# The place of the v projection in slot 3 of a transformer layer on TensorE

## What is computed

```python
q = (route @ wq + bq).reshape(b_, r_, k_, H, D)
k = (route @ wk + bk).reshape(b_, r_, k_, H, D)
v = (route @ wv + bv).reshape(b_, r_, k_, H, D)
scores = jnp.einsum('brkhd,brnhd->brknh', q, k) / D ** 0.5
attn = jax.nn.softmax(scores, axis=3)
out = jnp.einsum('brknh,brnhd->brkhd', attn, v).reshape(b_, r_, k_, m_)
out = out @ wo + bo
x = _layernorm(route + out, ln1_g, ln1_b)
ff = jax.nn.relu(x @ w1 + b1) @ w2 + b2
return _layernorm(x + ff, ln2_g, ln2_b)
```

## Time and profile before

| | |
|---|---|
| runs of the kernel | 4436.37, 4440.16, 4438.13 us; median 4438.13 us |
| the profiled execution | 4437.33 us, its span 4435.3 us |
| mean granted TensorE clock | 0.990 of full speed |
| TensorE busy, matmuls | 97% of the span |
| TensorE busy, weight loads | 85% |
| VectorE busy | 85% |
| GpSimd busy | 81% |
| ScalarE busy | 77% |

### The profile page before, as it was taken

How to read it: one execution, slowest core, us unless ns; L and a number is a source line. 1 busy time by engine, 2 the same in 40 slices (tenths; PEclk the granted TensorE clock), 3 DMA queues, 4 the chain that set the end, 5 groups by cost and what they waited for, 6 DMA issues and landing times.

```text
span 4435.3 us, 151196 instructions
## 1 busy us (share of the span) xinstructions
PE 4316.3 (97%) x51984; PEld 3791.2 (85%) x51984; DVE 3748.7 (85%) x9739; ACT 3417.8 (77%) x5889; POOL 3613.0 (81%) x4620
## 2 busy tenths in 40 slices
PE   4999999999999999999999999999999999999998
PEld 4888888888888888888888888888888888888886
DVE  4888888888888888888888888888888888888886
ACT  2777777777777777777778777877777777777776
POOL 4788888878888888788888878888887888888887
PEclk7999999999999999999999999999999999999999
DMA  4444444444444444444444444444444444444442
GB/s 110 122 129 129 125 131 126 130 120 131 125 129 128 129 130 124 124 129 129 126 131 125 131 121 131 126 130 129 127 130 119 128 130 128 126 131 127 130 126 60
DMA packets 756258, 555.92 MB, mean 125 GB/s; under 512 B 95872, under 2 KB 755328, under 8 KB 755456
## 3 DMA queue, kind: packets, MB, share of 16 engines
q1 hardware_dynamic: 755456, 545.81, 45.6%
HBM read 69.47 MB, written 67.11 MB: 31 GB/s over the span
## 4 chain that ended last, share of the span: by engine, by line
PE 75%; issue 13%; DVE 6%; ACT 3%; SPq 2%; DMA 1%; DVEq 0%; POOL 0%; ACTq 0%; POOLq 0%
PE oT_ps L697 11%; PE bankB L656 10%; PE bankC L656 10%; PE bankC L635 10%; PE s_ps L670 9%; PE sT_ps L684 8%; PE bankA L710 5%; PE bankA L765 5%; DVE rest_sb L468 5%; PE bankB L635 4%; ACT nT_parts L425 3%; PE bankA L629 2%; SPq L238 1%; DMA stack<-parts 1%; SPq L210 0%
## 5 line engine op out<-in xcount | busy, mean ns | idle before, releaser
L390 ACT ACTIVATE prob_sb<-sT_ps 128x1024 f32<-128x1024 f32 x1024 | 1049.5, 1025 | 770.8 <-PE sT_ps L684 753.6
L498 DVE TENSOR_REDUCE max_sb<-s_ps 128x8 f32<-128x1024 f32 x1024 | 1230.5, 1202 | 24.8 <-PE s_ps L670 14.8
L263 POOL TENSOR_TENSOR parts<-rest_sb,parts 128x512 bf16<-128x512 f32 x512 | 584.1, 1162 | 266.0 <-ACT parts L364 266.0
L670 PE MATMUL s_ps<-stack 96*128 96x128 bf16 x8192 | 638.5, 221 | 31.3 <-issue 15.0
L670 PEld LDWEIGHTS s_ps<-stack 96*128 96x128 bf16 x8192 | 485.3, 98 | 209.8 <-issue 178.7
L684 PE MATMUL sT_ps<-stack 99*128 99x128 bf16 x8192 | 629.1, 219 | 1.3 <-ACT prob_sb L390 1.3
L697 PE MATMUL oT_ps<-prob_sb,v_ones 128*32 128x128 f32 x16384 | 554.0, 276 | 2.2 <-ACT prob_sb L390 2.2
L656 PE MATMUL bankB<-w_sb,h_sb 128*128 128x128 f32 x4096 | 513.1, 278 | 2.4 <-ACT h_sb L371 2.4
L684 PEld LDWEIGHTS sT_ps<-stack 99*128 99x128 bf16 x8192 | 504.3, 98 | 3.0 <-ACT prob_sb L390 1.8
L656 PE MATMUL bankC<-w_sb,h_sb 128*128 128x128 f32 x4096 | 499.2, 275 | 0.0
L635 PE MATMUL bankC<-nT_parts,w_parts 128*128 128x512 f32 x1536 | 467.0, 412 | 27.2 <-DVE rest_sb L468 4.9
(11 more groups left out here) (80 smaller groups left out, 9321.4 us busy)
## 6 DMA issues: line engine op xcount, KB each, us to landing
stack<-parts SPq DMA_DIRECT2D x3072, 128.0 KB, 2.4
x_sb<-in_x SPq DMA_DIRECT2D x256, 256.0 KB, 3.0
out<-out_sb SPq DMA_DIRECT2D x256, 256.0 KB, 2.3
stack<-max_parts SPq DMA_DIRECT2D x768, 8.0 KB, 1.9
w_sb<-in_L_conv_w SPq DMA_DIRECT2D x2, 256.0 KB, 3.1
be_row<-in_L_conv_ln_b SPq DMA_DIRECT2D x2, 256.0 KB, 19.9
g_row<-in_L_conv_ln_g SPq DMA_DIRECT2D x2, 256.0 KB, 22.7
bo_row<-in_L_conv_bo SPq DMA_DIRECT2D x1, 256.0 KB, 8.7
```

What stands on the lines that cost most here:

```text
L263: pool.tensor_tensor(parts[:, r % 2, 3 * c + LO], rest_sb[:, c], parts[:, r % 2, 3 * c + MID], ALU.subtract).then_inc(lo_split, 1)
L390: act.activation(prob_sb[:, s % 2], sT_ps[:], ACT.Exp, scale=float(D) ** -0.5).then_inc(exp_done, 1)
L498: dve.reduce_max(max_sb[:, (r - lag) % 2, :, s], s_ps[:].rearrange("p (h k) -> p h k", h=H), AX.X).then_inc(max_done, 1)
L670: ins = pe.matmul(s_ps[:, h * P:(h + 1) * P], stack[0:PROD, (r - lag) % 4, 0, h, tok], stack[0:PROD, (r - lag) % 4, 1, h, tok], start=True ...
```

## The change

In slot 3 the projection of v is written between the two chunks of the feed-forward, where it stood behind both. Nothing else differs; in the changed kernel v's products have the line 764 in place of 765.

```diff
--- before.py
+++ after.py
@@ -757,7 +757,6 @@
                                  ident[:]).then_inc(maxT_done, 1)
                 if live(t, r, 5):
                     hidden(t, r, 5, 0)
-                    hidden(t, r, 5, 1)
                 if live(t, r, 0):
                     pe.wait_ge(xT_joined, upto(t, r, 0, plus=1))
                     pe.wait_ge(rest_made, upto(t, r, 0, per=2, plus=1))
@@ -765,6 +764,8 @@
                         ins = pe.matmul(A[:, s * P:(s + 1) * P], xT_sb[:, s * P:(s + 1) * P],
                                         wv_sb[:], start=True, stop=True)
                     ins.then_inc(v_done, 1)
+                if live(t, r, 5):
+                    hidden(t, r, 5, 1)
                 if live(t, r, 3):
                     if live(t, r, 2):
                         pe.wait_ge(max_parts_made, upto(t, r, 2, plus=1))
```

## The result

| | before | changed |
|---|---|---|
| median of the runs | 4439.15 us (4436.37 to 4445.43, 4 runs) | 4361.82 us (4358.52 to 4365.66, 4 runs) |
| the profiled execution | 4437.33 us | 4365.66 us |
| its span | 4435.3 us | 4363.6 us |

The ratio is 0.9824 with a 95% interval of 0.9807 to 0.9841: 77 us faster. Forecast were 4350 us and a gain of 88.

A forecast was written before the change was run, and what follows sets the result against it. TensorE bounds the kernel, waiting at h1 for VectorE's remainder of k. 247 x 0.39 = 96 us less 8 for late landings is 88, so 4437.33 becomes 4349, plus 0.8: 4350 us; forecast range 4330 to 4372, 80% range 4322 to 4388.

The forecast's parts named there:

- h1's wait: TensorE, second feed-forward chunk: the remainder of k ends 0.45 us ahead of it, so its wait goes whole.
- v's own waits: TensorE, v between the chunks: remainder of q done some 0.3 us ahead, joined x over 4 us; no wait.
- The price of the wait: TensorE, first chunk's loads to attend's: 2.86 us with the wait, 2.49 without, so 0.37 us a step.
- Boundaries: TensorE, new changeovers v to h1 and h1 to attend: h0 to attend 2.47 us, gain 0.39 a step, bounds 0.10 and 0.49.
- The 0.02 taken off because of L710's row: h0 to attend taken as 2.47, not 2.49 us: v-shaped group to chunk shows no idle time before its loads.
- The upper bound of 2.76: h0 to attend, if h1 to attend costs the largest idle time after such a product, 0.27 us.
- What is late next: Spare left: slot 0's scores 0.20 us, x's transposes 0.21, h1's relu 0.1; late stack landings give back 8 us.
- the bubble was hidden anyway: Rival: h1's wait costs only the matmul rows' 4.9 us in all, giving 4433 us; chance 0.04.
- A wait takes its place: Rival: z, the maximum or landings hold TensorE in most steps; 0.2 us a step left, 4389 us; chance 0.13.
- The full gain: Rival: loads at both new boundaries hide behind running products; 0.49 us a step, about 4317 to 4325; chance 0.08.
- slower by a new boundary: Rival: TensorE's changeovers v to h1 and h1 to attend cost more than the bubble; 4463 us; chance 0.03.
- Both signs of failure: Wrong if z or L498 ends TensorE's idle time in most steps, or 0.3 us idle precedes h1 or attend.

The follow-up runs named there:

- e5: Kernel before, v still behind both chunks, with q and k exchanged on every engine so k comes first: 4354.55 us, ratio 0.9812.
- e6: Changed kernel with v ahead of both feed-forward chunks instead of between them: 4451.64 us, ratio 1.0032.
- e7: e1 with one filler memset a step on VectorE ahead of the row maximum of slot 3: 4356.03 us.
- e1: Changed kernel with the six stacking DMAs of the high parts issued early, ahead of the row maxima's DMAs: 4341.82 us, ratio 0.9779.
- e2: Kernel before with the six stacking DMAs of the high parts issued early, ahead of the row maxima's DMAs: 4429.39 us, ratio 0.9979.
- e4: Changed kernel without the middle and low parts of the row maxima's split, three VectorE instructions a step fewer: 4341.57 us, ratio 0.9777.

## Why the prediction was right, and where its sizes were off

The forecast of 4350 us missed the median of 4361.82 by 12, inside its range, with the sign and the mechanism it named. The ends of that range are looser than the prediction says: by its own terms, gains of 0.30 and 0.45 a step with 0 to 24 us of DMA lateness give 4388 and 4327, not 4372 and 4330. The measured time lies inside either.

1. *h1's wait* and *v's own waits*: right. The remainder of k was forecast 0.45 us ahead of h1 and was 0.57; v has no idle time before it. e5 shows that the gain comes with the wait gone and v in its old place, and e6 that v must not come before the remainder of q.

2. *The price of the wait.* Read from two neighbouring steps at 0.37 us, with the matmul row's 4.9 us and the load row's 134.3 us set aside. The loads now give 2.86 - 2.48 = 0.38, the chain 16.83 - 16.48 = 0.35 for the whole step. Behind attend the ordinary loads stand where they stood but for one hundredth (attend to L710's loads: 1.86 before, 1.87 now); over 500 to 4000 us the medians of h0 to attend are 2.85 and 2.49, so the 0.38 of two single steps is a little large. What the prediction cites there tells how near TensorE is to its limit. It prices no wait, and neither row was the price of this one.

3. *Boundaries*: mis-sized by a little. I took 2.47 and then a gain of 0.39 for the whole step; the order is worth 0.01 at most (e5), the step gains 0.35. That is 247 x 0.04 = 10 us of the 11 that were missing. The 0.02 taken off because of L710's row had no ground. The upper bound of 2.76 was far off, and the row, the same work in the same 2.49 us, was right. The Trainium skill's rule that loads are pulled ahead of running matmuls (TensorE: Matmul & The Clock Gate, Step-by-step), which would have given 0.49 a step, does not show here: attend's narrow loads start 0.37 us after the last load of h1, at 3012.03, when h1's products are all but through (the chain has them until 3012.10). The page ties the rule to row groups that do not conflict, or to the background weight buffer; no row here shows whether either held.

4. *What is late next*: all right in kind. The maximum was forecast 0.20 us ahead of slot 0's scores; the profile has 0.22, and e7's filler measures 0.21. z has 0.29, forecast 0.21. The stack's lateness was put at 8 us back, 20 steps of 0.4; e1 and e2 together show 10.5, and the table 18 waits of 10.4 us behind the first 200 us.

Sum with the measured terms: 247 x 0.35 = 86, less 10.5: 76, against 77 measured. The two terms that were off, 0.39 for 0.35 and 8 for 10.5, lean the same way. The agreement to 1 us is closer than the terms allow: 0.01 us a step is 2.5 us, and the medians of the kernel before differ by 1.9 us between sets.

Of the rivals, *the bubble was hidden anyway* falls with the result. *A wait takes its place* is true only for the landings and at 10.5 us; for VectorE it is not yet true, with 0.2 us in hand. *The full gain* and *slower by a new boundary* fall with 2.48 us from h0 to attend.

Both signs of failure that the prediction named came up, and both were badly chosen. The first was that L498 ends TensorE's idle time in most steps; the table now has that row 249 times, 60.0 us, where it had 39. But the idle time itself is the same 0.20 us before the scores of slot 0 as in the earlier trace rows, where it is called "issue". The maximum now ends 0.22 us ahead of these loads instead of 0.59, near enough for the profile to name it, and e7 shows that it is not yet what the loads wait for.

The second was an idle time of 0.3 us or more before attend; there are 0.37 us, put down to the maxima, and e4 shows that the maxima are not what it waits for. By the rows it is the time in which h1's wide products run out before attend's narrow loads start; no run changed the width of either, so this reading is not shown. With v ahead of attend, as in e5, only 0.12 us lie between the last of v's loads and attend's.

What stays open: why landings scatter as they do was not tried, nor why e5 is faster than the changed kernel (4354.55 against 4361.82 us, 5 us when each is held against its own runs of the kernel before). Late landings are not the answer: the matmul row of e5 has 20 waits for the stack, 16.0 us, against 23 and 22.1, and most of that difference is in the filling. What e4's three removed instructions on VectorE are worth was not taken apart from the earlier DMAs.

The fastest version that leaves nothing out is e1, the change with the high parts' DMAs early: 4341.82 us, 2.2% faster than the kernel before.

## What to carry to other kernels

Price a wait by two like stretches, one with it and one without, between the same two places on the engine; the idle time in front of the waiting row was too long here (0.53 us for 0.37) and that of the matmul rows far too short. To move a piece of ready work into a bubble, look at what it needs itself: between the chunks it was free, one place earlier it brought its own wait of the same length. And a bubble on the engine that bounds the kernel also absorbs the scatter of what feeds it; when it is closed, make the feeding side earlier too, which here was worth a quarter of the gain again.

## What the runs showed of the hardware

- The loads of attend (128x32, from v_ones) start 0.37 us after the last load of a chunk of wide products: with the signal of the maxima 0.34 us ahead (the changed kernel), with it 0.9 us earlier still (e4), and in e6. The time is not lost, since h0 to attend is 2.48 us there and 2.49 with 0.12 us of it (e5).
- The twelve DMAs of the stack took SyncE 7.7 us to issue in a step of the kernel before, 8.2 in one of the changed kernel and 8.9 in one of e4, and 2.4 us to land at the median. With some 1 us in hand between the last landing and its use, by the prediction's estimate, the matmul row of the changed kernel has 23 waits for them in 256 steps, 22.1 us. With six of them issued more than 5 us earlier (from 3008.28, where the changed kernel's twelve start at 3013.65) one wait of 0.7 us is left (e1).
